# A banded attention chain on one core: narrow heads woven between their wide head's chunks, all scores in strips, and one query and key stack for the narrow heads

## The reference, cut to what matters

```python
scores = jnp.einsum('bqhd,bkhd->bhqk', q, k) / math.sqrt(head_dim)
bias = -jnp.abs(pos[None, :] - pos[:, None]).astype(jnp.float32)
scores = scores + slopes[None, :, None, None] * bias[None, None]
probs = jax.nn.softmax(scores, axis=-1)
out = jnp.einsum('bhqk,bkhd->bqhd', probs, v).reshape(B, L, D)
```

## Time and profile before

| | |
|---|---|
| three runs | 1064.97, 1067.75, 1069.89 us |
| profiled execution, its own time | 1069.68 us |
| its span | 1067.9 us (1.8 us less than its own time) |
| TensorE busy, share of the span | 1023.5 us, 96% |
| ScalarE busy | 812.4 us, 76% |
| ScalarE's exponentials in the attention | 489, busy 660.9 us |
| VectorE and GpSimd busy | 452.8 and 321.3 us |

### The profile page before, as it was taken

The page is one execution under the profiler, slowest core; times in us unless marked ns, Lnnn a source line. Parts: engine busy times, 40 slices in busy tenths (PEclk is TensorE's granted clock), DMA queues, the critical chain, the costliest instruction groups (busy, mean ns, idle before and its releaser), DMA issues. The chain is left out here.

```text
span 1067.9 us, 37330 instructions
## 1 busy us (share of the span) xinstructions
PE 1023.5 (96%) x16398; PEld 712.1 (67%) x16398; DVE 452.8 (42%) x1064; ACT 812.4 (76%) x807; POOL 321.3 (30%) x486
## 2 busy tenths in 40 slices
PE   9999899999999999999999999999996389999997
PEld 6555576766676776877756766868685346666665
DVE  5778334464342432225354723324257511111165
ACT  3564799999999999999999999999966164111252
POOL 3333122134121121112231721211330345554443
PEclk9999999999999999999999999999999589999999
DMA  5765312212222111112342121220209246544473
GB/s 186 219 198 167 115 56 75 60 60 73 58 59 63 51 46 46 49 45 72 95 116 62 56 73 51 57 60 20 87 21 307 40 124 173 124 114 112 113 281 136
DMA packets 76550, 104.67 MB, mean 98 GB/s; under 512 B 13774, under 2 KB 62556, under 8 KB 76380
## 3 DMA queue, kind: packets, MB, share of 16 engines
q1 hardware_dynamic: 65852, 87.94, 26.4%
q0 software_dynamic: 6080, 9.06, 4.1%
q10 hardware_dynamic: 4448, 5.19, 1.5%
HBM read 66.49 MB, written 31.48 MB: 92 GB/s over the span
## 5 line engine op out<-in xcount | busy, mean ns | idle before, releaser
L1037 ACT ACTIVATE prob<-ps 128x1536 f32<-128x1536 f32 (+5 forms) x489 | 660.9, 1520 | 13.4 <-PE ps L993 12.1
L993 PE MATMUL ps<-q_stack,k_stack 123*32 123x512 bf16 (+18 forms) x7784 | 454.6, 314 | 4.2 <-ACT prob L1037 2.3
L1017 PE MATMUL ps<-prob,v_head 128*32 128x128 f32 (+7 forms) x7288 | 455.2, 338 | 0.0
L993 PEld LDWEIGHTS ps<-q_stack,k_stack 123*32 123x32 bf16 (+3 forms) x7784 | 243.8, 96 | 138.7 <-ACT prob L1037 72.7
L1017 PEld LDWEIGHTS ps<-prob,v_head 128*32 128x32 f32 x7288 | 284.4, 109 | 57.3 <-issue 6.9
L1051 POOL TENSOR_TENSOR prob<-prob,near_bias 128x128 f32<-128x128 f32 x288 | 141.6, 496 | 500.9 <-ACT prob L1037 498.2
L1051 DVE TENSOR_TENSOR prob<-prob,near_bias 128x128 f32<-128x128 f32 x288 | 97.3, 345 | 401.5 <-ACT prob L1037 400.1
L1070 DVE RECIPROCAL o_rec<-o_den 128x128 f32<-128x128 f32 x128 | 113.8, 924 | 0.7
L1827 ACT ACTIVATE hT<-ps 128x512 f32<-128x512 f32 x28 | 16.7, 596 | 109.7 <-PE ps L1750 105.1
L1750 PE MATMUL ps<-xeT,w 128*128 128x512 f32 x224 | 99.4, 601 | 0.8 <-issue 0.7
L1764 PE MATMUL ps<-w,hT 128*128 128x256 f32 x448 | 99.0, 382 | 0.0
(11 more groups left out here) (175 smaller groups left out, 613.8 us busy)
## 6 DMA issues: line engine op xcount, KB each, us to landing
qk_parts<-split SPq DMA_DIRECT2D x32, 384.0 KB, 3.2
w<-L_ffn_experts_inter_dram SPq DMA_DIRECT2D x7, 1024.0 KB
w<-n_L_ffn_experts_out_dram SPq DMA_DIRECT2D x7, 1024.0 KB
q_stack<-qk_parts SPq DMA_DIRECT2D x31, 192.0 KB
k_stack<-qk_parts SPq DMA_DIRECT2D x31, 192.0 KB
z_rows<-v SPq DMA_DIRECT2D x8, 516.0 KB, 8.5
heads<-o_out SPq DMA_DIRECT2D x128, 32.0 KB, 2.4
v<-in_L_attn_x_dram SPq DMA_DIRECT2D x8, 512.0 KB, 7.6
```

Of the source, the lines that this page charges most:

```text
L993: mm = pe.matmul(ps[k:k + keys, SLOT_BANKS * (c % 2) + bank, col:col + z - a], k_st[n % STACKS][0:rows, kb * P + k:kb * P + k + keys], q_s ...
L1017: mm = pe.matmul(ps[32 * g:32 * g + 32, 6 + n % 2, column:column + width * times], vh[n % 2][:, kb, :], moving, start=(n, g) not in begun, ...
L1037: act.activation(prob[:, c % RING, 0:at + z - a], ps[:, bank:bank + SLOT_BANKS, :].rearrange("p c n -> p (c n)")[:, 0:at + z - a], ACT.Exp ...
```

## The change

It edits the order and the packing of the attention's chunks, and what hangs on them:

1. `packed` goes; `woven` takes its place. A wide item and its narrow item are packed as a pair: the wide item's chunks come in order, and from its fifth chunk on the narrow item's chunks are put between them at even distances, ending before the wide item's last four chunks. `evenly` makes the narrow item's chunks of about equal width, so that some are narrower than 1536 columns. No chunk is shared with the next pair. There are 494 chunks with 747,584 columns in place of 489 with 748,256.
2. All scores are in strips, and `pv` of chunk c-4 stands behind the scores of every chunk c.
3. `stack_of`: wide items alternate between stack pairs 0 and 1, all narrow items use pair 2. The load of item n waits for the last scores of the item that used the same pair before.
4. `place_of`: the PSUM bank and the `v_head` buffer of an item; `RANK` and `ENDING`: the outputs are taken, divided and stored in the order in which the items end, the narrow one three chunks ahead of its wide one.
5. The second four of the bias additions stand at fixed distances from the end.

With the new functions, a narrow item (odd n) ends and the next narrow item (n+2) begins at these chunks:

| narrow items | last chunk of the one to first chunk of the next, in chunks |
|---|---|
| 1 to 3, 3 to 5, 17 to 19, 19 to 21 | 10 |
| 5 to 7, 7 to 9, 9 to 11, 21 to 23, 23 to 25, 25 to 27 | 9 |
| 11 to 13, 13 to 15, 27 to 29, 29 to 31 | 8 |
| 15 to 17 | 14 |

The first narrow item begins at chunk 10 (before: 20). For wide items the pair's user before is two pairs back.

```diff
-def packed(items):
...
+def evenly(n, h, at):
+
+    columns = at + sum(z - a for _, a, z in spans(h, 0))
+    count = -(-columns // WIDTH)
+    widths = range(-(-columns // count // 16) * 16, WIDTH, 16)
+    return fill(n, h, at, 0, next((w for w in widths if w >= at and len(fill(n, h, at, 0, w)) == count), WIDTH))
+
+
+def woven(wide, narrow):
+
+    first = fill(*wide, 0, 0)
+    at = sum(z - a for *_, a, z, _ in first[-1])
+    second = evenly(*narrow, at)
+    wide_chunks, narrow_chunks = first[:-1], [first[-1] + second[0]] + second[1:]
+    chunks, done = [], 0
+    for r, chunk in enumerate(wide_chunks):
+        chunks.append(chunk)
+        due = max(0, r + 2 - NARROW_FROM) * len(narrow_chunks) // (len(wide_chunks) - NARROW_FROM - 2)
+        chunks += narrow_chunks[done:due]
+        done = max(done, due)
+    return chunks
...
-CHAIN = packed(ITEMS)
+CHAIN = [chunk for n in range(0, len(ITEMS), 2) for chunk in woven((n, ITEMS[n][1]), (n + 1, ITEMS[n + 1][1]))]
...
+ENDING = sorted(range(len(ITEMS)), key=lambda n: LAST[n])
+RANK = [ENDING.index(n) for n in range(len(ITEMS))]
+def place_of(n):
+    return (n // 2 + n % 2) % 2
+def place_user_before(n):
+    earlier = [m for m in range(len(ITEMS)) if place_of(m) == place_of(n) and LAST[m] < FIRST[n]]
+    return max(earlier, key=lambda m: LAST[m]) if earlier else None
+def stack_of(n):
+    return 2 if n % 2 else n // 2 % 2
+def stack_users_before(n):
+    return [m for m in range(n) if stack_of(m) == stack_of(n)]
...
-BIAS_AT = [FIRST[-8] + 3 * c for c in range(QG)] + [FIRST[-1] + 3 * c for c in range(QG)]
-def scores_in_strips(c):
-    return ITEMS[items_of(c)[0]][1] >= IN_STRIPS
+BIAS_AT = [FIRST[-8] + 3 * c for c in range(QG)] + [CHUNK_COUNT - 13 + 3 * c for c in range(QG)]
...
-        due = c - VALUE_LAG + 1 if scores_in_strips(c) or c % 2 == 1 else done
+        due = c - VALUE_LAG + 1
...
-            n = LAST.index(slot - VALUE_LAG - 2)
+            n = RANK[LAST.index(slot - VALUE_LAG - 2)]
...
-            if n >= STACKS:
-                sp.wait_ge(scored, LAST[n - STACKS] + 1)
+            if stack_users_before(n):
+                sp.wait_ge(scored, LAST[stack_users_before(n)[-1]] + 1)
...
-                    pe.wait_ge(stack_in[n % STACKS], (n // STACKS + 1) * 16 * (LOADS + 1))
+                    pe.wait_ge(stack_in[stack_of(n)], (len(stack_users_before(n)) + 1) * 16 * (LOADS + 1))
...
-                    keys = 32 if scores_in_strips(c) else P
-                    for k in range(0, P, keys):
+                    for k in range(0, P, 32):
...
-                    if n >= 2:
-                        pe.wait_ge(o_read, n - 1)
+                    if place_user_before(n) is not None:
+                        pe.wait_ge(o_read, RANK[place_user_before(n)] + 1)
...
-            dve.wait_ge(pv_done, LAST[n] + 1)
+            dve.wait_ge(pv_done, LAST[ENDING[n]] + 1)
...
-                if n >= 2:
-                    pool.wait_ge(pv_done, LAST[n - 2] + 1)
+                if place_user_before(n) is not None:
+                    pool.wait_ge(pv_done, LAST[place_user_before(n)] + 1)
```

More of the change, by code:

```diff
@@ L48 @@
 VALUE_LAG = 4
-IN_STRIPS = 5
 ONE_SIDED, ONE_SIDED_ONCE = 2, 4
 STACKS = 3
+NARROW_FROM = 4
 ST = CAP // P
@@ L936, in store_turned_heads @@
         def store_turned_heads(n):
-            b, h = ITEMS[n]
+            b, h = ITEMS[ENDING[n]]
             sp.wait_ge(o_ready, n + 1)
@@ L947, in banded_sync @@
                 continue
-            k = n % STACKS
+            k = stack_of(n)
             if (b, h) == ITEMS[H]:
@@ L990, in score @@
                     bank, col = divmod(at, CH)
-                    keys = 32 if scores_in_strips(c) else P
-                    for k in range(0, P, keys):
-                        mm = pe.matmul(ps[k:k + keys, SLOT_BANKS * (c % 2) + bank, col:col + z - a],
-                                       k_st[n % STACKS][0:rows, kb * P + k:kb * P + k + keys],
-                                       q_st[n % STACKS][0:rows, a:z], start=True, stop=True,
+                    for k in range(0, P, 32):
+                        mm = pe.matmul(ps[k:k + 32, SLOT_BANKS * (c % 2) + bank, col:col + z - a],
+                                       k_st[stack_of(n)][0:rows, kb * P + k:kb * P + k + 32],
+                                       q_st[stack_of(n)][0:rows, a:z], start=True, stop=True,
                                        skip_group_check=True)
@@ L1016, in pv @@
                     moving = slab[:, at:at + width]
-                mm = pe.matmul(ps[32 * g:32 * g + 32, 6 + n % 2, column:column + width * times],
-                               vh[n % 2][:, kb, :], moving, start=(n, g) not in begun, stop=False,
+                mm = pe.matmul(ps[32 * g:32 * g + 32, 6 + place_of(n), column:column + width * times],
+                               vh[place_of(n)][:, kb, :], moving, start=(n, g) not in begun, stop=False,
                                skip_group_check=True)
@@ L1055, in take @@
         def take(n):
-            dve.wait_ge(pv_done, LAST[n] + 1)
+            dve.wait_ge(pv_done, LAST[ENDING[n]] + 1)
             if n >= 2:
                 dve.wait_ge(o_ready, n - 1)
-            dve.tensor_copy(o_sb[n % 2][:, :], ps[:, 6 + n % 2, :]).then_inc(o_read, 1)
+            dve.tensor_copy(o_sb[n % 2][:, :], ps[:, 6 + place_of(ENDING[n]), :]).then_inc(o_read, 1)
         def spread(n):
@@ L1101, in banded_gpsimd @@
                 b, h = ITEMS[n]
-                if n >= 2:
-                    pool.wait_ge(pv_done, LAST[n - 2] + 1)
-                pool.tensor_copy(vh[n % 2][:, :, 0:HD], t["v"][:, b * KB:(b + 1) * KB, h * HD:(h + 1) * HD])\
+                if place_user_before(n) is not None:
+                    pool.wait_ge(pv_done, LAST[place_user_before(n)] + 1)
+                pool.tensor_copy(vh[place_of(n)][:, :, 0:HD], t["v"][:, b * KB:(b + 1) * KB, h * HD:(h + 1) * HD])\
                     .then_inc(vh_done, 1)
```

## The result

The changed kernel takes 1156.05 us (median of 4 runs, 1153.45 to 1158.63) beside 1066.86 for the one before (4 runs): a ratio of 1.0824, 95% interval 1.0802 to 1.0846, or +89 us. The forecast was +58 us and 1126, with 1146 as the upper end of its range. Its kind was right, its size was not. The profiled execution took 1158.26 us with a span of 1156.3, 88.4 more than before.

The account below looks back on a forecast made before the run. It took ScalarE's exponentials, 1.331 us a chunk, to bound the attention, with TensorE close behind. -15.3 + 57.1 + 1.5 + 12 + 3.2 = +58.5 us on 1069.68 gave 1128.2, in the median's terms 1126 us; range 1102 to 1146.

Parts of the forecast that it names:

- weave and strips: In the attention, ScalarE's 21.6 us of loss falls to 6, with 0.3 for added chunks: -15.3 us.
- wait of narrow heads for their stack: Before narrow heads' first scores, TensorE waits for the stack load and ScalarE stands still: +57.1 us, bounds 0 to 72.
- wide stacks and x rows: One or two wide loads may be late, and x rows slow items 21 and 23: +1.5 us, 0 to 6.
- clock: TensorE's clock falls in ten of the stack waits, those at k = 9 and 8: +12 us, 0 to 23.
- end: Behind the last values, VectorE needs 8.7 us instead of 5.5 until the output projection: +3.2 us, 0 to 5.
- 15.3 us: Length of a stack load from issue to end of transfers, read from item 15's, set against each narrow head's room.
- at nothing: New places of banks and value buffers, and the same eight bias additions, were said to cost no time.
- I take 1.2 us each: Cost of each of ten clock falls in the stack waits, from 3.3 us at half clock: 12 us in all.
- the fall comes 4 to 5 us after the stop: TensorE's clock drops 4 to 5 us after it goes idle, so only waits of 4.2 to 5.5 us count.
- Rival B: Stack waits come, but waits of 4 to 5 us may not lower TensorE's clock: 1114 us, chance 0.27.
- rival C: In the attention, the weave gives nothing and the loss stays 21.6 us: 1141 us, chance 0.12.
- Rival A: Before narrow heads' first scores, the load is hidden if below about 11 us on average: 1056 us, chance 0.08.

Follow-up runs that it names:

- the dummy work: Changed kernel with 11 to 28 unread TensorE matmuls ahead of the stack wait of each of the fourteen narrow heads that waited long: 1137.11 us, ratio 1.0616.
- the no-strips run: Changed kernel with split loads and narrow heads ending six chunks ahead, heads 0 to 4 using one 128-key matmul instead of four strips: 1077.04 us, ratio 1.0053.
- the cured versions: Changed kernel with stack loads split into 17 DMAs: 1068.31 us; the same with narrow heads also ending six chunks ahead instead of three: 1061.43 us.

## Why the prediction came out as it did

| term | forecast, us | found, us | from |
|---|---|---|---|
| weave and strips | -15.3 | -11 | loss elsewhere 11.9 for 22.8 |
| wait of narrow heads for their stack | +57.1 | +71.2 | loss at their first chunks (1.5 of it the PSUM bank at item 25) |
| wide stacks and x rows | +1.5 | +2.0 | items 20 and 22 |
| clock | +12 | +23 | 23.1 behind the waits, 22 by the dummy work |
| end | +3.2 | +4.2 | last values to last product, 9.8 for 5.6 |
| sum | +58.5 | +89 | measured +89 |

**The mechanism** was right in its main parts: place, releaser and number of the waits (item 17, k = 14, does not wait: 0.1 us), and the order by k: 4.0 us on average at k = 10, 4.9 at 9, 5.8 at 8. The sizes of two terms were wrong. The room was exact: from issue to need the fourteen loads had 155.6 us in all (summed from their records), by my figures 4 x 12.5 + 6 x 11.1 + 4 x 9.8 = 155.8.

**The first step that failed** is "15.3 us" as the length of every load. It came from item 15's in the kernel before. The fourteen loads took 14.7 to 18.9 us, 16.0 on average, so 0.7 x 14 = 10 us more. This could have been read before the run: in the trace of the kernel before the same fourteen loads take 14.7 to 20.0 us, 16.0 on average, and items 21 and 23 are the longest there too (20.0 and 18.7). I read two of them. Items 21 and 23 (18.9 and 18.7) make seven of the ten; I had seen that the x rows lengthen them and had put that at no more than a part of 1.5 us. With the x rows moved away both take 16.1. I also took 0.2 us off each wait as ScalarE's spare. That holds where the clock was still full when the wait ended (items 3, 5, 7 and 9: ScalarE lost 0.16 us less than TensorE waited, on average); where it had fallen by then ScalarE lost some 0.3 us more, as the first scores run at half clock. Together 70.9 for 55.6, and 0.3 for 1.5 at item 1. The sum stayed inside its bound of 72. About 1.5 of the 70.9 belong to the bias additions at item 25, which the prediction had "at nothing".

**The second** is "I take 1.2 us each": ten falls of the clock at 1.2 us. There were thirteen, and they cost 1.8 us each. The count failed at "the fall comes 4 to 5 us after the stop": here it came 2.1 to 4.9 us after TensorE's last work. Even item 3's wait of 2.95 us brought one, item 5's of 2.81 did not. The size failed at the 3.3 us that I had taken as the length of the lower clock, from the earlier trace rows; here it stood at half for 3.4 to 10.2 us, and in the item 15 case 5.7 us of this lay behind the wait. 23 was my own upper bound. The Trainium skill (TensorE: Matmul & The Clock Gate, HAM oscillation), which I weighed and set aside, lets every such wait start at the lower clock. Nine of the fourteen did; behind four more (items 3, 7, 9 and 25) the clock fell 0.3 to 0.9 us after TensorE had begun again. So the trace agrees with it more than with my ten.

**The range** failed for a reason of its own, and it doesn't follow from its parts. Rival B less 7 is 1107 and rival C plus 10 is 1151, not 1102 and 1146; the load's own upper bound lies 15 us above my value (72 for 57.1), not 10. The clock's upper bound, 11 us above my value, was not in it, though I had worked it out. With the load at 16.3 and the clock at 23 the sum gives 1126 + 15 + 11 = 1152, a little under the 1156 measured. Terms that rest on one cause (longer waits bring more falls) err together.

**Two readings of room were off**, without weight in the sum. Between a wide head and the user of its pair before lie 26 to 41 chunks, not 29 to 34; items 20 and 22, the two that waited, have 27 and 28. And "twenty or more chunks" of room for each load in the kernel before holds for the buffer (24 to 40 chunks), but not for the load: SyncE issued those of items 4 and 20 only some 18 us ahead of the first exponential.

**The weave** gave 11 us of the 15.3 amid the waits. Rival C (it gives nothing) is refuted. The argument against it, that heads 5 to 7 in strips lose little, was only half of the reason: strips alone leave most of the loss (20.0 us for 22.8), and the no-strips run shows that the weave alone loses what the strips win. Rival A (load hidden, 1056 us) is what the cured versions show from the other side: with loads of 9.5 to 12.9 us the same change gives 1068, with room added 1061. Its threshold, 11 us on average, was near. Rival B (no clock) is the dummy-work run in essence: 1137.

**The end** cost 4.2 for 3.2: of the narrow head's division one quarter of four came before the wide head's copy, as foreseen, but it ran until 0.5 us behind the last values; 0.46 us of idle time stand behind the first product, and the last product took 0.85 us for 0.69. 8.7 + 1.1 = 9.8.

## What to carry to other kernels

Before buffers are handed out anew, write down for each the room that a load then has (chunks between the last use and the next first use, times the cadence) and set it against the length of the load from issue to landing, the worst one too: here 9.8 to 12.5 us of room against 16 us turned a hidden load into 70 us of waits and 23 us of lower clock. The cure needs no more memory: a shorter load (here by splitting DMAs of few, large outermost steps into ones of 16 rows), or a few chunks more of room; a further buffer helps only if the queue that issues the load isn't itself standing in a wait. And two changes that are worth nothing or less by themselves (strips, weave) can be worth 1% together (0.9907 once the waits were cured), so a failed bundle is taken apart before it is dropped.

## What was not expected of the hardware

The strips: the same scores of heads 0 to 4 as four matmuls of 32 keys each instead of one of 128 keys, 17,478 matmuls in the kernel instead of 15,858, are worth 15.6 us where wide and narrow chunks alternate, and nothing where they don't (ratio 1.0006, 0.9997 to 1.0016). Why the weave needs them isn't shown by these runs. And a load of one stack, the same rows, takes 16.5 us as eleven DMAs and 10.2 us as seventeen whose outermost dimension is larger. Last, VectorE's small multiply (0.29 us) lasts up to 2.0 us when it meets a 2.2 us addition on GpSimd: in the traces of the kernels before and after and of two variants 18 multiplies took over 0.9 us, and all 18 end 0.15 us behind such an addition.
